# Attention 0: the order of values and scores in each unit of TensorE's program

## The chip, the cores and the metric

The kernel runs on one core of a Trainium2 chip. The metric is the device time of one execution in microseconds (us). The core has five engines that work side by side, each through its own list of instructions in order: TensorE (PE; its weight loads are shown apart as PEld), VectorE (DVE), ScalarE (ACT), GpSimd (POOL) and SyncE (SP), which only issues transfers. They wait for one another by semaphores.

## What is computed

Four layers act on `x` of 8 batches, 256 rows and 1024 columns: a cross attention with 32 heads and 8 key heads (attention 0), a linear layer with low-rank updates, a second cross attention and a linear layer in 8 bits. Only the first matters here. Its core, cut down:

```python
def _L0_xattn_ref(hidden_states, encoder_hidden_states, wq, wk, wv, wo, ln_w):
    x = _rmsnorm(hidden_states, ln_w)
    q = jnp.einsum('bqd,hd->bqh', x, wq).reshape(B, Qlen, N_HEADS, HEAD_DIM)
    k = jnp.einsum('bkd,hd->bkh', encoder_hidden_states, wk).reshape(B, Klen, N_KV_HEADS, HEAD_DIM)
    v = jnp.einsum('bkd,hd->bkh', encoder_hidden_states, wv).reshape(B, Klen, N_KV_HEADS, HEAD_DIM)
    ...
    scores = jnp.einsum('bhqd,bhkd->bhqk', q, k) / np.sqrt(HEAD_DIM).astype(np.float32)
    attn = jax.nn.softmax(scores.astype(jnp.float32), axis=-1).astype(q.dtype)
    out = jnp.einsum('bhqk,bhkd->bhqd', attn, v)
    ...
    return jnp.einsum('bqh,dh->bqd', out, wo)

x = x + jnp.tanh(g_xattn[0]) * _L0_xattn_ref(_layernorm(x, axis=-1), ctx_4096, ...)
```

## The kernel before

The program runs in stages, one behind the other: context (keys, values), attention 0 (`attn0_stage`), the output projection and first linear layer (`mid_stage`), attention 1, and the last linear layer. Attention 0 occupies about 181 to 688 us.

**Units.** Each batch has 16 units (`UNITS`): four heads (`t = n // 2`) times one half of the 256 rows (`qb = n % 2`). A unit goes through the engines in this way:

- scores (L956): TensorE multiplies queries with keys, 4 matmuls into the bank pair `n % 2` of `a_psS`;
- `maximum` (L1063): VectorE takes the negated row maximum of each head out of those banks;
- `exponentials` (L1148): ScalarE takes four exponentials, with their sums, into `a_prob`;
- `transposes` (L966): TensorE transposes the probabilities, 8 of 128x128, into `a_psT`; ScalarE (L1165) and in some units VectorE (L1108) copy them to `a_probT`;
- `values` (L979): TensorE multiplies them with the values into `a_psO`, 8 matmuls that the profile shows as 16 records. Each fills only 32 columns of the array. Behind the values of every odd unit come two more transposes (L985), which turn the reciprocals of the sums; GpSimd (L881) spreads these beforehand;
- `normalise_o` (L1076, L1078): VectorE multiplies the two and frees `a_psO` by `o_ready`, for which the values of the next even unit wait.

**The query step.** Each unit also carries a piece of the next batch's queries: in units 0 to 3 four transposes of x (L915), and from unit 4 on a half or a whole query tile of 12 or 24 matmuls (L931). All of them use the one bank `a_psQ`. VectorE empties it in a `split` of two instructions (L1056 and L1058: high and low part). Before it writes the bank again, TensorE waits for the second (`psQ_lo`). In the last batch no next one exists; the matmuls of the low-rank update stand there (L1006, from unit 4 on), with VectorE's `copy_update` (L1094) after each of four quarters.

**The order.** It is written out by hand, and each engine keeps it. TensorE in unit n of a batch, before:

```python
transposes(b, n)
if n + 2 < UNITS:
    scores(b, i, u, n + 2)
...
if n:
    values(b, u, n - 1)
if more:
    query_step(b + 1, 1 - u, n)
```

So scores run two units ahead and values one behind. VectorE's step n holds, in this order: the split (in step 0 the last of this batch; in steps 1 to 4, 5, 7, 8, 10, 11, 13 and 14 the next batch's), in odd steps from 5 the copy L1108, in odd steps the reciprocals L1113, `maximum(n + 2)`, in even steps `normalise_o(n // 2 - 1)`. While batches remain whose x is still to come (batches 0 to 5), step 6 adds the statistics of one tile (L590), step 9 the rest of them (L590, L607) and step 12 the normalisation (L644). In the last batch, each even step adds the low part of an output weight (L1068) instead, and steps 7, 10 and 13 a `copy_update` at their end. ScalarE's step n holds the copies of unit n and then the exponentials of unit n + 2.

Two batches stand in one round of a hardware loop of three rounds; the last two batches stand behind it.

Of the kernel before, what the change touches and what calls it, by code (L numbers as in the profile page):

```python
# [690 lines left out]
def attn0_stage(nc, sh, c, scratch, wq, rows, norm):  # L691
# [22 lines left out]
    with ExitStack() as es:  # L714
# [186 lines left out]
        def _(pe):  # L901
# [35 lines left out]
            def query_step(b, u, n):  # L937

                if n < XFILLS:
                    transposed_x(b, u, n)  # L940
                    return
                three, part = (n - XFILLS) // 3, (n - XFILLS) % 3
                if part == 0:
                    query(b, 2 * three, range(KT))
                else:
                    query(b, 2 * three + 1, range((part - 1) * KT // 2, part * KT // 2))

            def scores(b, i, u, n):

                t, qb = n // TT, n % TT  # L950
                if n % (UNITS // 2) == 0:
                    pe.wait_ge(q_stacked[t // QUAD], 16 * QUAD_DMAS * (b + 1) + 1)
                if n == 0:
                    pe.wait_ge(kv_loaded[u], 16 * 5 * (i + 1))
                for j in range(JH0):
                    last = nc.tensor.matmul(psS[:, 2 * (n % 2) + j // 2, (j % 2) * S:(j % 2 + 1) * S],  # L956
                                            q_stack[:, t, j, qb * P:(qb + 1) * P],
                                            k_stack[:, u, (t // REP0) * JH0 + j, :], start=True, stop=True)
                last.then_inc(scores_full, 1)

            def transposes(b, n):
                pe.wait_ge(exp_done, UNITS * b + n + 1)
                for kt in range(TT):
                    pe.wait_ge(psT_copied[kt], UNITS * b + n + 1)
                    for j in range(JH0):
                        last = nc.tensor.transpose(psT[:, kt, j * P:(j + 1) * P],  # L966
                                                   prob[:, n % 2, j, kt * P:(kt + 1) * P], ident[:, :])
                    last.then_inc(psT_full[kt], 1)

            def values(b, u, n):  # L970
                t, qb = n // TT, n % TT
                if qb == 0:
                    pe.wait_ge(o_ready, KT * b + t + 1)
                for kt in range(TT):
                    pe.wait_ge(psT_copied[kt], UNITS * b + n + 2)
                for kt in range(TT):
                    for j in range(JH0):
                        head = (t // REP0) * JH0 + j
                        nc.tensor.matmul(psO[j * HD0:(j + 1) * HD0, 0, qb * P:(qb + 1) * P],  # L979
                                         v0[:, u, kt, head * HD0:(head + 1) * HD0], probT[:, n % 2, kt, j, :],  # L980
                                         start=(kt == 0), stop=(kt == TT - 1))
                if qb == TT - 1:
                    pe.wait_ge(recip_ready, KT * b + t + 1)
                    for s in range(TT):
                        last = nc.tensor.transpose(psO[:, 1, s * P:(s + 1) * P],  # L985
                                                   recip[:, t % 2, s, :, :].rearrange("p j c -> p (j c)"), ident[:, :])
                    last.then_inc(psO_full, 1)
# [9 lines left out]
            def update_part(quarter, kt):  # L997

                if kt == 0:
                    if quarter == 0:  # L1000
                        pe.wait_ge(summed, 1)
                        pe.wait_ge(psQ_lo, Q_USES * B + 1)
                    else:
                        pe.wait_ge(update_copied, quarter)
                    pe.wait_ge(table_loaded[quarter % 2], 32 * (quarter // 2) + 32)
                last = nc.tensor.matmul(psQ[0:RR, 0:QUARTER], wsum[:, kt, :], table(quarter, kt // QUAD)[:, kt % QUAD, :],  # L1006
                                        start=(kt == 0), stop=(kt == KT - 1))
                if kt == KT - 1:
                    last.then_inc(update_full, 1)
# [5 lines left out]
            def body(i, final):  # L1015
                for u in range(2):
                    b = 2 * i + u
                    more = not (final and u == 1)
                    for n in range(UNITS):
                        transposes(b, n)  # L1020
                        if n + 2 < UNITS:
                            scores(b, i, u, n + 2)
                        elif more:
                            scores(b + 1, i + u, 1 - u, n + 2 - UNITS)
                        if n:
                            values(b, u, n - 1)
                        if more:
                            query_step(b + 1, 1 - u, n)
                        else:
                            for quarter, kt in update_steps.get(n, ()):  # L1030
                                update_part(quarter, kt)
                    values(b, u, UNITS - 1)

            with pe.Fori(0, PAIRS - 1) as i:
                body(i, False)
            body(PAIRS - 1, True)

        @block.vector
# [1437 lines left out]
```

## Time and profile before

| | us |
|---|---|
| median of 3 runs | 1495.08 |
| lowest and highest | 1495.05, 1495.64 |
| the profiled execution | 1496.8 |
| span of its instructions | 1495.1 |
| mean granted TensorE clock, share of full speed | 0.966 |

| engine | busy, us | share of the span |
|---|---|---|
| PE | 1377.2 | 92% |
| PEld | 1120.8 | 75% |
| DVE | 971.4 | 65% |
| ACT | 745.9 | 50% |
| POOL | 426.3 | 29% |

The views name an instruction by engine, line of the kernel and operation, then what it writes and what it reads (`a_psS<-a_k_stack,a_q_stack`), the shapes and the count. Matmuls are pipelined, and their ends in the trace are modelled: one that follows closely starts before the one ahead has ended, so on TensorE the distance from start to start is what counts. Busy time is a union over records and hides this. Where an engine was idle, the releaser is inferred from semaphore events.

### The profile page before, as it was taken

To read this page: it belongs to the slowest core of one execution; us is meant where nothing else is said; L and a number is where in the kernel's file an instruction comes from. 1 tells how busy PE (TensorE), PEld (TensorE's weight loads), DVE (VectorE), ACT (ScalarE), POOL (GpSimd) and SP (SyncE) were. 2 spreads that over 40 slices of the span, in tenths; PEclk is the share of its full clock that TensorE was granted. 3 is DMA by queue.
4 is the path that set the end of the run, shared out by engine and by line. 5 is a ranking of instruction groups with operands and counts; after the bars stand their busy time and mean duration, and the time that the engine had idled before them with its cause. 6 is when DMAs were issued, how large, how long until landed. Compare 5 with 4: busy or idle time off the path is not lost. (4 is left out here: it accounts for less than half of the span.)

```text
span 1495.1 us, 28528 instructions
## 1 busy us (share of the span) xinstructions
PE 1377.2 (92%) x10782; PEld 1120.8 (75%) x10782; DVE 971.4 (65%) x1564; ACT 745.9 (50%) x1881; POOL 426.3 (29%) x473
## 2 busy tenths in 40 slices
PE   6998789989989999987999999999779999999388
PEld 6998778979889898865888888888556666666144
DVE  4363277777767767565232256578567999998597
ACT  4231167766757767763111110113157777777396
POOL 0010001101010110010110232232358888887324
PEclk9999889999999999999999999999889999999789
DMA  6742454553544536464445452112332222221023
GB/s 224 244 155 85 90 126 117 139 146 77 145 110 120 147 96 167 125 197 150 166 167 197 157 210 99 56 36 84 113 81 65 62 64 64 63 64 43 1 85 141
DMA packets 127910, 174.93 MB, mean 117 GB/s; under 512 B 27799, under 2 KB 96919, under 8 KB 127792
## 3 DMA queue, kind: packets, MB, share of 16 engines
q1 hardware_dynamic: 127792, 173.26, 39.9%
q8 instruction: 86, 1.41, 0.4%
q14 instruction: 32, 0.26, 0.1%
HBM read 86.94 MB, written 35.29 MB: 82 GB/s over the span
## 5 line engine op out<-in xcount | busy, mean ns | idle before, releaser
L1148 ACT ACTIVATE a_prob<-a_psS,a_negmax 128x256 f32<-128x256 f32 x512 | 236.7, 483 | 158.6 <-DVE a_negmax L1063 158.4
L1063 DVE TENSOR_REDUCE a_negmax<-a_psS 128x4 f32<-128x1024 f32 x128 | 154.1, 1204 | 68.1 <-PE a_psS L956 66.5
L881 POOL COPY a_recip<-a_recip_head 128x256 f32<-128x256 f32 x64 | 25.6, 400 | 526.5 <-DVE a_recip_head L1113 526.5
L931 PE MATMUL a_psQ<-a_xT_hi,wide 128*128 128x256 f32 x912 | 170.9, 288 | 0.4
L1375 PE MATMUL m_psY<-wide,m_a_hi 128*128 128x512 f32 x512 | 159.3, 393 | 6.8 <-DVE m_a_lo L1423 6.8
L1375 PE MATMUL m_psY<-w_ffn,m_a_hi 128*128 128x512 f32 x512 | 158.3, 390 | 0.0
L966 PE MATMUL a_psT<-ident,a_prob 128*128 128x128 f32 x1024 | 138.0, 279 | 14.1 <-issue 6.1
L931 PEld LDWEIGHTS a_psQ<-a_xT_hi,wide 128*128 128x128 f32 x912 | 138.7, 189 | 9.1 <-issue 5.9
L1165 ACT COPY a_probT<-a_psT 128x512 f32<-128x512 f32 x208 | 115.8, 609 | 36.7 <-PE a_psT L966 35.6
L966 PEld LDWEIGHTS a_psT<-ident,a_prob 128*128 128x128 f32 x1024 | 116.7, 143 | 23.0 <-issue 12.7
L931 PE MATMUL a_psQ<-a_xT_lo,wide 128*128 128x256 f32 x456 | 127.5, 280 | 0.0
L1375 PEld LDWEIGHTS m_psY<-wide,m_a_hi 128*128 128x128 f32 x512 | 96.8, 189 | 27.5 <-DVE m_a_lo L1423 7.0
L1375 PEld LDWEIGHTS m_psY<-w_ffn,m_a_hi 128*128 128x128 f32 x512 | 95.6, 188 | 19.5
L1148 ACT ACTIVATION_READ_ACCUMULATOR a_prob<-a_psS,a_negmax 128x1 f32 x512 | 109.4, 214 | 0.0
L2115 ACT ACTIVATE b_prob<-b_prob 128x1024 f32<-128x1024 f32 x64 | 67.9, 1061 | 79.1 <-DVE b_prob L1989 79.1
L1375 PE MATMUL m_psY<-wide,m_a_lo 128*128 128x512 f32 x256 | 100.2, 392 | 0.0
L1375 PE MATMUL m_psY<-w_ffn,m_a_lo 128*128 128x512 f32 x256 | 99.7, 389 | 0.0
L956 PE MATMUL a_psS<-a_k_stack,a_q_stack 128*128 128x256 f32 x512 | 94.1, 307 | 2.9 <-issue 2.9
L1983 DVE TENSOR_REDUCE b_maxes<-b_psS 128x16 f32<-128x1024 f32 x64 | 77.9, 1217 | 27.1 <-PE b_psS L1891 26.0
L1901 PEld LDWEIGHTS b_psT<-ident,b_prob 128*128 128x128 f32 x512 | 60.2, 142 | 35.2 <-issue 32.9
L931 PEld LDWEIGHTS a_psQ<-a_xT_lo,wide 128*128 128x128 f32 x456 | 85.7, 188 | 0.0
L1820 POOL TENSOR_TENSOR b_halves<-b_prob 128x512 f32<-128x512 f32 x64 | 82.5, 1290 | 6.6 <-ACT b_prob L2115 6.0
(233 smaller groups left out, 3013.9 us busy)
## 6 DMA issues: line engine op xcount, KB each, us to landing
a_q_stack<-a_q_hi SPq DMA_DIRECT2D x128, 128.0 KB, 2.6
a_q_stack<-a_q_lo SPq DMA_DIRECT2D x128, 128.0 KB, 2.6
c_raw<-lay_ctxT SPq DMA_DIRECT2D x16, 512.0 KB, 4.8
rows<-in_x SPq DMA_DIRECT2D x8, 1024.0 KB, 6.4
scratch_o<-a_oT SPq DMA_DIRECT2D x16, 512.0 KB, 3.0
m_x<-in_x SPq DMA_DIRECT2D x8, 1024.0 KB, 5.9
scratch_x<-m_x SPq DMA_DIRECT2D x8, 1024.0 KB, 5.1
b_q_stack<-b_q_hi SPq DMA_DIRECT2D x64, 128.0 KB, 2.3
```

The source lines that it names most:

```text
L881: nc.gpsimd.tensor_copy(recip[:, t % 2], recip_head[:, t % 2].unsqueeze(3).broadcast_to([P, TT, JH0, HD0])).then_inc(recip_ready, 1)
L931: last = nc.tensor.matmul(bank[:, 0:S], w[:, kt, t * P:(t + 1) * P], a[:, kt, :], start=(kt == 0 and w is wq.hi and a is xT_hi), stop=(kt ...
L956: last = nc.tensor.matmul(psS[:, 2 * (n % 2) + j // 2, (j % 2) * S:(j % 2 + 1) * S], q_stack[:, t, j, qb * P:(qb + 1) * P], k_stack[:, u, ...
L966: last = nc.tensor.transpose(psT[:, kt, j * P:(j + 1) * P], prob[:, n % 2, j, kt * P:(kt + 1) * P], ident[:, :])
L1063: nc.vector.tensor_reduce(negmax[:, n % 2, :], psS[:, bank:bank + 2, :].rearrange("p a (j k) -> p (a j) k", k=S), AX_X, ALU.max, negate=Tr ...
L1148: last = nc.scalar.activation(prob[:, n % 2, j, :], psS[:, 2 * (n % 2) + j // 2, (j % 2) * S:(j % 2 + 1) * S], ACT.Exp, bias=negmax[:, n % ...
L1165: nc.scalar.copy(probT[:, n % 2, kt, :, :], psT[:, kt, :].rearrange("p (j q) -> p j q", j=JH0)).then_inc(psT_copied[kt], 1)
L1375: last = nc.tensor.matmul(psY[:, 2 * t + h, :], a[:, u, kt, rows_t], m[:, kt, cols], start=(kt == 0 and a is a_hi and m is w.hi), stop=(kt ...
L1820: nc.gpsimd.tensor_tensor(halves[:, n % 2], unit[:, :, 0:NK1 // 2], unit[:, :, NK1 // 2:NK1], ALU.add).then_inc(halves_ready, 1)
L1901: last = nc.tensor.transpose(psT[:, t, j * P:(j + 1) * P], prob[:, n % 2, (4 * t + j) * P:(4 * t + j + 1) * P], ident[:, :])
L1983: nc.vector.tensor_reduce(maxes[:, n % 2, :], psS[:, n % 2, :].rearrange("p (h k) -> p h k", h=NH1), AX_X, ALU.max).then_inc(max_ready, 1)
L2115: nc.scalar.activation(prob[:, n % 2, :], prob[:, n % 2, :], ACT.Exp).then_inc(exp_done, 1)
```

## The change

In every unit except the first of each batch (which has no values) TensorE now runs the values of the unit one back ahead of the scores of the unit two on. Nothing else is touched; all semaphore counts stay.

```diff
                     for n in range(UNITS):
                         transposes(b, n)
+                        if n:
+                            values(b, u, n - 1)
                         if n + 2 < UNITS:
                             scores(b, i, u, n + 2)
                         elif more:
                             scores(b + 1, i + u, 1 - u, n + 2 - UNITS)
-                        if n:
-                            values(b, u, n - 1)
                         if more:
                             query_step(b + 1, 1 - u, n)
                         else:
```

TensorE's list in unit 6 of a batch in the loop, an even unit, where the two transposes of reciprocals go along with the values. The rows named ISA and REGISTER_ALU are waits and their counting.

```order
 L962 REGISTER_ALU
 L966 MATMUL a_psT<-ident,a_prob 128x128 x8
+L979 MATMUL a_psO<-a_probT,a_v 32x128 x8
+L985 MATMUL a_psO<-ident,a_recip 128x128 x2
 L952 ISA
 L956 MATMUL a_psS<-a_k_stack,a_q_stack 128x256 x4
-L979 MATMUL a_psO<-a_probT,a_v 32x128 x8
-L985 MATMUL a_psO<-ident,a_recip 128x128 x2
 L931 MATMUL a_psQ<-a_xT_hi,wide 128x256 x2
 L931 MATMUL a_psQ<-a_xT_lo,wide 128x256
```

The scores, with the wait for the stacked queries in front of them, now stand behind the values and the reciprocals, and directly ahead of the query step.

TensorE's list in unit 7, an odd unit, which starts a new query tile:

```order
 L962 REGISTER_ALU
 L966 MATMUL a_psT<-ident,a_prob 128x128 x8
-L956 MATMUL a_psS<-a_k_stack,a_q_stack 128x256 x4
 L973 REGISTER_ALU
 L979 MATMUL a_psO<-a_probT,a_v 32x128 x8
+L956 MATMUL a_psS<-a_k_stack,a_q_stack 128x256 x4
 L925 REGISTER_ALU
 L931 MATMUL a_psQ<-a_xT_hi,wide 128x256 x2
```

The scores have moved behind the values and behind the wait for `o_ready` (L973) in front of those. The lists of the other engines are the same as before.

## Rows read from the trace of the kernel before

**Rows 1.** Busy time by engine, batch 5 from unit 1 on; clock, DMA at the end.
```profile
505.98:564.74 58.76, 58.14 (x658) 52.18 (x657) 42.75 (x74) 42.51 (x151) 5.62 (x15) 1.00 0.51 130
```

**Rows 2.** Waits of TensorE's loads, 195 to 690 us: total, times, longest.
```profile
PEld a_psQ L1006 <- DVE a_update L1094: 6.1, 3, 2.9
...
PEld a_psQ L931 <- DVE a_q_lo L1058: 3.2, 12, 0.3
```

**Rows 3.** Timeline of TensorE, batch 5, unit 6: start us, duration us, instruction.
```profile
523.04 0.39 PE L931 MATMUL a_psQ<-a_xT_hi,wide 128*128 128x256 f32 x2
...
524.18 0.71 PE L956 MATMUL a_psS<-a_k_stack,a_q_stack 128*128 128x256 f32 x4
524.82 0.64 PE L979 MATMUL a_psO<-a_probT,a_v 128*32 128x128 f32 x16
525.40 0.44 PE L985 MATMUL a_psO<-ident,a_recip 128*128 128x128 f32 x2
525.59 0.50 PE L931 MATMUL a_psQ<-a_xT_hi,wide 128*128 128x256 f32 x2
```

**Rows 4.** Timeline of TensorE, other joints: batch 5, unit 6; batch 7; batch 2, unit 0.
```profile
523.82 0.60 PE L966 MATMUL a_psT<-ident,a_prob 128*128 128x128 f32 x4
...
680.14 0.60 PE L966 MATMUL a_psT<-ident,a_prob 128*128 128x128 f32 x4
680.67 0.64 PE L979 MATMUL a_psO<-a_probT,a_v 128*32 128x128 f32 x16
...
316.78 0.72 PE L956 MATMUL a_psS<-a_k_stack,a_q_stack 128*128 128x256 f32 x4
317.34 0.27 PE L915 MATMUL a_psQ<-ident,rows 128*128 128x128 f32 x1
```

**Rows 5.** Timeline of TensorE, batch 5, unit 7: values and start of the query.
```profile
528.52 0.65 PE L979 MATMUL a_psO<-a_probT,a_v 128*32 128x128 f32 x16
529.09 0.39 PE L931 MATMUL a_psQ<-a_xT_hi,wide 128*128 128x256 f32 x1
```

**Rows 6.** Timeline of VectorE, batch 5, steps 6 and 7; idle time in brackets.
```profile
524.93 1.23 DVE L1063 TENSOR_REDUCE a_negmax<-a_psS 128x4 f32<-128x1024 f32 x1 [2.07 <-PE a_psS L956]
...
526.52 0.42 DVE L1078 TENSOR_TENSOR a_oT<-a_psO,a_recipT 128x256 f32<-128x256 f32 x1
...
528.50 0.42 DVE L1058 TENSOR_TENSOR a_q_lo<-a_psQ,a_q_hi 128x256 fp32r<-128x256 f32 x1
```

**Rows 7.** Timelines of VectorE and TensorE, batch 5, units 12 and 13.
```profile
549.35 1.22 DVE L1063 TENSOR_REDUCE a_negmax<-a_psS 128x4 f32<-128x1024 f32 x1 [2.18 <-PE a_psS L956]
...
553.17 0.42 DVE L1058 TENSOR_TENSOR a_q_lo<-a_psQ,a_q_hi 128x256 fp32r<-128x256 f32 x1
...
553.65 0.50 PE L931 MATMUL a_psQ<-a_xT_hi,wide 128*128 128x256 f32 x2
```

**Rows 8.** Timelines of VectorE and TensorE, batch 5, units 2 and 3.
```profile
510.72 1.22 DVE L1063 TENSOR_REDUCE a_negmax<-a_psS 128x4 f32<-128x1024 f32 x1 [0.32 <-PE a_psS L956]
...
513.37 0.69 DVE L1058 TENSOR_TENSOR a_xT_lo<-a_psQ,a_xT_hi 128x512 fp32r<-128x512 f32 x1
...
514.11 0.66 PE L915 MATMUL a_psQ<-ident,rows 128*128 128x128 f32 x4
```

**Rows 9.** Timelines of VectorE and TensorE, batch 5, unit 10.
```profile
540.38 0.42 DVE L1058 TENSOR_TENSOR a_q_lo<-a_psQ,a_q_hi 128x256 fp32r<-128x256 f32 x1
...
541.38 0.48 PE L931 MATMUL a_psQ<-a_xT_hi,wide 128*128 128x256 f32 x2
```

**Rows 10.** The exponentials, from the page's costliest groups: busy us, mean ns, idle.
```profile
L1148 ACT ACTIVATE a_prob<-a_psS,a_negmax 128x256 f32<-128x256 f32 x512 | 236.7, 483 | 158.6 <-DVE a_negmax L1063 158.4
```

**Rows 11.** Timeline of VectorE, batch 7, steps 6 and 7.
```profile
646.08 1.23 DVE L1063 TENSOR_REDUCE a_negmax<-a_psS 128x4 f32<-128x1024 f32 x1 [2.27 <-PE a_psS L956]
...
650.94 0.40 DVE L1094 TENSOR_SCALAR a_update<-a_psQ 40x256 f32<-40x256 f32 x1
```

**Rows 12.** Busy time around the start of batch 4; the granted clock is third last.
```profile
441.00:444.30 3.30, 2.88 (x14) 2.91 (x15) 0.05 (x1) 1.17 (x2) 0.00 (x0) 0.50 0.86 243
445.00:505.00 60.00, 59.18 (x667) 53.03 (x664) 43.84 (x77) 43.60 (x154) 5.62 (x15) 1.00 0.44 110
```

## The prediction

> **What bounds the kernel now.** I read three views of the stretch from 181 to 688 us, in which attention 0 runs its 128 units. First the busy table of one batch, 505.98 to 564.74 us [rows 1]. TensorE's matmuls fill 58.14 of 58.76 us. VectorE has 42.75 and ScalarE 42.51, so each is idle for some 16 us. TensorE is the bound, and nothing else is. Work that is only moved on TensorE costs nothing there; what can cost is a new idle stretch on it. Second the list of waits of TensorE's loads [rows 2]: it waits for VectorE in a few short places, among them for `a_q_lo` (12 times, 3.2 us) and, in the last batch, for `a_update` (3 times, 6.1 us). So VectorE has little time in hand somewhere. Third the timeline around those places, where the reader should look at the gap between the end of the releasing VectorE instruction and the start of the waiting matmul.
>
> Names: T(n), S(n+2), V(n-1), R and Q(n) are the transposes of the probabilities, the scores, the values, the two transposes of reciprocals behind every second V, and the query step. Unit n of a batch ran T, S, V, (R), Q and will run T, V, (R), S, Q. R stands where n is even. Batches are 0 to 7; the rows below are of batch 5 unless another is named.
>
> **The cost on TensorE itself.** The parts are the same; the joints between them change. T into S: S starts at 524.18 [rows 3] and the last four transposes at 523.82 [rows 4], 0.36 us ahead. T into V: the same four start 0.53 us ahead of V (680.14 to 680.67, in a unit without scores) [rows 4]. So T into V costs 0.17 more. S into V is 0.64 from start to start, V into R 0.58, R into Q 0.19 [rows 3], V into Q 0.57 (528.52 to 529.09) [rows 5]. S into a query step, which no unit of the steady state had, is seen once a batch in unit 0, where nothing stands between: 316.78 to 317.34, 0.56 [rows 4]. An even unit from S's old place to Q's start: before 0.64 + 0.58 + 0.19 = 1.41; after 0.17 + 0.58 + 0.19 + 0.56 = 1.50. That is 0.09 more, but the first pair of query matmuls takes 0.50 us behind V or R and 0.39 behind matmuls of its own kind [rows 3], and S is of that kind: 0.11 back. Sum: nothing, with bounds of 0.1 us on either side for each of 111 units, or 11 us. I take zero, since the same two joints (out of a transpose, out of V) remain in number and only their neighbours change.
>
> The Trainium skill ("TensorE: Matmul & The Clock Gate", Part 3, The mechanism) says that a weight load overlaps matmuls in flight only where it goes to another row group. V's loads fill 32 columns over all rows, and the joint of 0.17 us is what that rule would give; by it the gap is moved and not removed, as in my sum.
>
> **What moves: the scores.** S starts later by what is now ahead of it. Even units: 0.17 + 0.58 + 0.19 = 0.94 us. Odd units: 0.17 + 0.57 = 0.74, and 0.02 for its own slower first matmul out of V, 0.76. V comes 0.64 - 0.17 = 0.47 earlier. No semaphore wait is added for V: T(n) waits for the same copies of the unit before. Behind S stands VectorE's row maximum (L1063), and VectorE works through its list in order: behind maximum(n+2) are queued, in even steps, `normalise_o`, statistics (step 6) or the normalisation (step 12), and then the split of the next step, for which the next Q waits. So a later maximum can stop TensorE one unit later. Unit by unit:
>
> Unit 6 into 7. The maximum of step 6 starts at 524.93, straight behind S, after 2.07 us of idle time; from there L1076, L1078, L590, L1056 and L1058 run without a gap until 528.50 + 0.42 = 528.92 [rows 6]. Q(7) starts at 529.09 [rows 5]: 0.17 in hand, of which a handoff needs 0.06 (next paragraph). The whole chain moves by 0.94. Cost 0.94 - 0.11 = **0.83 us**.
>
> Unit 12 into 13. Maximum at 549.35 behind S (2.18 idle), then the normalisation, and the split ends at 553.17 + 0.42; Q(13) starts at 553.65, at once [rows 7]. This is already a wait, so nothing is in hand: **0.94 us**.
>
> Unit 2 into 3. Maximum at 510.72 behind S (0.32 idle), the split ends at 513.37 + 0.69 = 514.06, Q(3) starts at 514.11 [rows 8]: **0.94 us**. Here V(2) also waits for `normalise_o` of that delayed step, with S(5) behind it. From there V and S take 0.06 + 0.57 + 0.56 = 1.19 us to Q(3), while VectorE's split takes two instructions of some 0.69, 1.4 us; so the split ends last and V's wait costs nothing more.
>
> Unit 9 into 10. The maximum of step 9 comes behind an odd unit's S, 0.76 later; the split ends at 540.38 + 0.42 = 540.80 and Q(10) starts at 541.38 [rows 9]: 0.58 - 0.06 = 0.52 in hand, cost **0.24 us**.
>
> All other units keep a margin. T's own wait for the exponentials is loose in the long units: maximum(8) ended at 526.16 [rows 6], four activations of 0.48 [rows 10] end by 528.1, and T(8) stands behind Q(7), which only starts at 529.09 and runs for some 2.8 us; 0.94 fits. In the short units 2 to 4 the exponentials are closer to their T, but the 0.94 us stall of unit 3 gives ScalarE the time back. The wait for `o_ready` ahead of V in odd units is the narrowest: `normalise_o` of step 6 ended at 526.52 + 0.42 = 526.94 [rows 6] and V began at 528.52 [rows 5], 1.58 apart; it shrinks by 0.94 + 0.47 = 1.41 to 0.17, and 0.06 is needed. It just holds.
>
> A stall of TensorE isn't made up, as TensorE is full. Per batch 0.83 + 0.94 + 0.94 + 0.24 = 2.95 us. Batches 0 to 5 have all four: 17.7. In batch 6 no x is left to normalise, so only the stall of unit 3 remains: 0.9.
>
> **Batch 7** has no query steps; the update's matmuls stand there, and each new quarter waits for VectorE's copy of the last. The maximum of step 6 waited 2.27 us for S and started at 646.08; behind it a queue without a wait ends with the copy at 650.94 + 0.40, where the quarter's matmuls, the next on TensorE, wait for it [rows 11]. The chain moves by 0.94; the same in units 10 and 13 (three waits of 6.1 us in all [rows 2]): 2.8 us. In its units 2 to 4, which have no query step to cover anything, I let a later S(4) delay T(4) through the exponentials by its whole 0.94; that is an estimate by the same figure, between nothing and 2 us. Together 3.8.
>
> Sum: 17.7 + 0.9 + 3.8 = 22.4 us in the stage, and the stages behind it start at its end. The profiled execution had 1496.8 us for a span of 1495.1; the median of the three runs, 1495.08, is 1.7 below its time. The added stalls don't depend on that offset, so 1495.1 + 22.4 = **1517.5 us**.
>
> **The clock.** From 441.0 to 444.3 us the granted clock was 0.50, the lower level of 1.2 GHz, at the start of the loop's third round; from 445 on it is 1.00 [rows 12]. 3.3 us at half speed can cost 1.65 at most. TensorE had stood idle just before, at the loop's turn. With the stage's idle stretches moved and lengthened, one or two such spells more or fewer are possible: 3 us on either side. The skill's page on the clock gate ("Why this matters for your kernels") warns of idle gaps of this length; by it the new stalls of under 1 us each leave the clock alone.
>
> **Rivals.**
> 1. *The joints on TensorE cost more than thought.* If S behind V and Q behind S cost 0.1 us a unit, the upper bound above, 111 units add 11 us: 1529. For it: no row shows V straight into S. Against: V into Q, V into R and S into a query step are all seen. Chance 0.10.
> 2. *VectorE catches up part of the delay.* If the maximum doesn't move by the full 0.94 or some queued work slips ahead of S, half the stalls remain: 1506. Against: every one of the four chains starts with VectorE idle and waiting for S, and its order is fixed. Chance 0.10. That nothing is seen at all would need margins near 0.9 us where [rows 5 to 8] show 0.17 us in hand and none: 1495, chance 0.03.
> 3. *Faster.* V behind T shares its joint, and S flows into Q without one. If T into V cost no more than T into S (0.17 saved) and S into Q saved another 0.12 through its warm pipeline, each of 111 units would gain 0.29 us, 32 in all, and with the 22.4 of stalls the result is 10 us faster, 1485. It decides from 0.2 us a unit. Against: the 0.53 us of [rows 4]. Chance 0.04.
>
> **How the numbers follow.** The forecast (1510 to 1526) has 0.73. Together with a part of rivals 1 and 2 the range that holds the time 8 times in 10 is 1508 to 1528: below are half of rival 2, no change and faster, above is half of rival 1. Measurements of this kernel can tell about 0.2%, 3 us, from no change. Slower by more: 0.73 + 0.10 + 0.10 = 0.93; same 0.03; faster 0.04.
>
> **What the changed profile would show.** S starts 0.94 (even) or 0.76 (odd) later behind T, V 0.47 earlier. TensorE's waits for `a_q_lo` and `a_xT_lo` grow by 0.8 to 0.9 us each in units 3, 7 and 13 of batches 0 to 5, and none appear in units 7 and 13 of batch 6. The period of units 8, 9, 11, 12, 14 is as before (within 0.1). The wait for `a_update` grows by 2.8. Matmul time of TensorE is unchanged. I am wrong if the waits stay and the units themselves lengthen (rival 1), if V of units 7, 9, 13 and 15 waits for `a_oT` by more than 0.1 us, or if the time comes from a later stage.

## The result and the profile after

The changed kernel takes 1519.92 us in the median (1518.44 to 1521.48), the one before 1495.07 (1494.56 to 1495.64). The ratio is 1.0166, with a 95% interval of 1.0149 to 1.0184: 24.9 us slower, where 22.4 were forecast. The profiled execution of the changed kernel had 1518.44 us and a span of 1516.7, which is 21.6 more than the span before. The three other executions of the changed kernel took 1.0 to 3.0 us longer, at a mean granted clock of 0.965 against 0.970 in the profiled one; what the traces below add up to belongs to the 21.6 and not to the 24.9. The matmuls of the stage behind attention 0 begin at 715.4 us in place of 693.4, 22.0 later, and at the end the spans differ by 21.6, so the whole loss lies in attention 0 and 0.4 us come back behind it.

TensorE's order in unit 6 and at the start of unit 7 of batch 5, from the timeline of the changed kernel (start, duration, instruction). It answers to [rows 3, 5]. In all views `...` stands for lines left out.

```profile
535.39 1.04 PE L966 MATMUL a_psT<-ident,a_prob 128*128 128x128 f32 x8
536.35 0.65 PE L979 MATMUL a_psO<-a_probT,a_v 128*32 128x128 f32 x16
536.93 0.44 PE L985 MATMUL a_psO<-ident,a_recip 128*128 128x128 f32 x2
537.12 0.72 PE L956 MATMUL a_psS<-a_k_stack,a_q_stack 128*128 128x256 f32 x4
537.68 0.40 PE L931 MATMUL a_psQ<-a_xT_hi,wide 128*128 128x256 f32 x2
...
539.10 1.03 PE L966 MATMUL a_psT<-ident,a_prob 128*128 128x128 f32 x8
540.06 0.65 PE L979 MATMUL a_psO<-a_probT,a_v 128*32 128x128 f32 x16
540.63 0.74 PE L956 MATMUL a_psS<-a_k_stack,a_q_stack 128*128 128x256 f32 x4
541.92 0.38 PE L931 MATMUL a_psQ<-a_xT_hi,wide 128*128 128x256 f32 x1 [0.55 <-DVE a_q_lo L1058]
```

Every joint (the time from the start of one kind of matmul to the start of the next) is as summed: transposes to values 0.96, values to reciprocals 0.58, reciprocals to scores 0.19, scores to query 0.56. The scores start 1.73 us behind the transposes of their unit; before it was 0.79. The first pair of query matmuls behind scores takes 0.40 us and not 0.50. Unit 6 as a whole lasts 3.71 us (535.39 to 539.10), and before 3.69. In unit 7 the bracket is the new thing: matmuls idle for 0.55 us until VectorE's `a_q_lo`, where [rows 5] had no bracket.

VectorE behind the later scores, in steps 6 and 7 of the same batch (compare [rows 6]):

```profile
537.88 1.23 DVE L1063 TENSOR_REDUCE a_negmax<-a_psS 128x4 f32<-128x1024 f32 x1 [2.45 <-PE a_psS L956]
...
539.47 0.42 DVE L1078 TENSOR_TENSOR a_oT<-a_psO,a_recipT 128x256 f32<-128x256 f32 x1
539.81 1.27 DVE L590 BATCH_NORM_STATS2 norm_stats<-rows 128x6 f32<-128x512 f32 x2
...
541.44 0.42 DVE L1058 TENSOR_TENSOR a_q_lo<-a_psQ,a_q_hi 128x256 fp32r<-128x256 f32 x1
```

The maximum starts 537.88 - 535.39 = 2.49 us behind the start of unit 6's transposes. Before, those began at 523.39 and the maximum at 524.93, 1.54 behind, which is 0.95 less than now. The split ends at 541.86 and TensorE goes on at 541.92. Step 12 and unit 13 show the same chain with the longer normalisation:

```profile
563.39 1.23 DVE L1063 TENSOR_REDUCE a_negmax<-a_psS 128x4 f32<-128x1024 f32 x1 [2.48 <-PE a_psS L956]
...
567.21 0.42 DVE L1058 TENSOR_TENSOR a_q_lo<-a_psQ,a_q_hi 128x256 fp32r<-128x256 f32 x1
...
567.69 0.51 PE L931 MATMUL a_psQ<-a_xT_hi,wide 128*128 128x256 f32 x2 [0.81 <-DVE a_q_lo L1058]
```

The list of waits of TensorE's loads over the stage (total, times, longest), answering to [rows 2]:

```profile
PEld a_psS L956 <- issue: 12.3, 62, 0.2
PEld a_psQ L931 <- DVE a_q_lo L1058: 11.9, 18, 1.0
PEld a_psO L979 <- DVE a_oT L1078: 11.4, 38, 1.0
PEld a_psQ L1006 <- DVE a_update L1094: 8.1, 3, 3.8
```

`a_q_lo` went from 3.2 us to 11.9: 18 waits are those of units 7, 10 and 13 of six batches. `a_update` went from 6.1 to 8.1, 2.0 us more and not the 2.8 of the forecast. The other two lines have to be read with care. The 62 waits of 0.2 us ahead of the scores are the joint behind the values, which stood ahead of the query before. Nearly all of the 38 on `a_oT` are the joint between transposes and values, laid to the semaphore that happened to be asked for there; TensorE's matmuls themselves wait for it 7 times, in unit 3 of batches 1 to 7 (below).

Start to start of transposes, changed kernel less the one before, in us, by unit of three batches without a disturbance of the clock at their start:

| unit | 2 | 3 | 4 | 7 | 8 | 10 | 13 | 14 | others | whole batch |
|---|---|---|---|---|---|---|---|---|---|---|
| batch 1 | 0.16 | 0.65 | -0.12 | 0.80 | -0.06 | 0.18 | 0.94 | -0.06 | 0.26 | 2.75 |
| batch 5 | 0.17 | 0.64 | -0.14 | 0.89 | -0.01 | 0.14 | 0.85 | -0.01 | 0.03 | 2.56 |
| batch 6 | 0.24 | 0.58 | -0.05 | 0.08 | -0.01 | 0.00 | 0.08 | 0.00 | 0.05 | 0.97 |

Units 3, 7, 10 and 13 carry the loss; what unit 2 adds, unit 4 mostly gives back. Over batches 0 to 6 it is 16.3 us in this trace, in batch 7 it is 7.1. The first unit had begun 1.5 us earlier than in the profile before, which leaves the 22.0 above. At the loop's turns the clock moved time about: unit 0 was 1.57 us longer in batch 2 and 1.38 shorter in batch 4.

### The profile page after: what moved, and what is told of

The parts are those of the page before. It is cut to its first block and busy times, and to the rows that moved or that the text cites. A ratio compares the mean times of both kernels' runs of the same rounds, so it can differ in the third digit from the quotient of the medians.

```text
span 1516.7 us, 28520 instructions
## 1 busy us (share of the span) xinstructions
PE 1379.9 (91%) x10774; PEld 1115.4 (74%) x10782; DVE 975.3 (64%) x1564; ACT 744.9 (49%) x1881; POOL 426.2 (28%) x473
## 5 line engine op out<-in xcount | busy, mean ns | idle before, releaser
L931 PE MATMUL a_psQ<-a_xT_hi,wide 128*128 128x256 f32 x912 | 163.6, 280 | 8.2 <-DVE a_q_lo L1058 8.1
L931 PEld LDWEIGHTS a_psQ<-a_xT_hi,wide 128*128 128x128 f32 x912 | 138.5, 188 | 11.9 <-DVE a_q_lo L1058 11.9
L966 PEld LDWEIGHTS a_psT<-ident,a_prob 128*128 128x128 f32 x1024 | 117.0, 144 | 24.9 <-issue 14.4
L931 PE MATMUL a_psQ<-a_xT_lo,wide 128*128 128x256 f32 x456 | 127.1, 279 | 0.0
L1148 ACT ACTIVATION_READ_ACCUMULATOR a_prob<-a_psS,a_negmax 128x1 f32 x512 | 104.6, 204 | 0.0
L979 PE MATMUL a_psO<-a_probT,a_v 128*32 128x128 f32 x2048 | 82.8, 280 | 4.4 <-DVE a_oT L1078 4.3
L931 PEld LDWEIGHTS a_psQ<-a_xT_lo,wide 128*128 128x128 f32 x456 | 85.6, 188 | 0.0
```

The source lines that it names most:

```text
L931: last = nc.tensor.matmul(bank[:, 0:S], w[:, kt, t * P:(t + 1) * P], a[:, kt, :], start=(kt == 0 and w is wq.hi and a is xT_hi), stop=(kt ...
L966: last = nc.tensor.transpose(psT[:, kt, j * P:(j + 1) * P], prob[:, n % 2, j, kt * P:(kt + 1) * P], ident[:, :])
L1148: last = nc.scalar.activation(prob[:, n % 2, j, :], psS[:, 2 * (n % 2) + j // 2, (j % 2) * S:(j % 2 + 1) * S], ACT.Exp, bias=negmax[:, n % ...
```

## The experiments

Each was timed beside the kernel before, on the same chip within a group. The ratios are to that kernel's runs. Medians of the kernel before were 1494.38 in the first group (experiments 1 to 4), 1494.04 in the second (5, 6, 7 and 9) and 1494.05 in the third (8 and 10). Of each kernel one execution has a trace.

**1. Values first everywhere but in four units.**

```diff
+values_first = n not in ((2, 6, 9, 12) if more else (2, 6, 10, 12))
+if n and values_first:
+    values(b, u, n - 1)
 if n + 2 < UNITS:
     scores(b, i, u, n + 2)
...
-if n:
+if n and not values_first:
     values(b, u, n - 1)
```

> The kernel before with the values put first in every unit except those whose scores start one of the four chains that ended in a stall: units 2, 6, 9 and 12 (2, 6, 10 and 12 in the last batch). 83 of 111 units with both parts are swapped. If the cost is VectorE's delayed queue, nearly all of the 24.9 us goes: 1496 to 1499 us, and TensorE's waits for a_q_lo are back near 3.2 us. If the joints between kinds of matmuls on TensorE cost it, three quarters stay: about 1513. If it is the values' own earlier place (their wait for a_oT), it stays too.

Measured: 1497.35 us, ratio 1.0013 (0.9998 to 1.0027). Nearly all of the loss is gone, though three quarters of the swaps are in. (Units with both parts are 118 and not 111 as forecast and expectation have it: 15 in each of seven batches and 13 in the last; 86 are swapped here.) In the trace 1.9 us are left. Most of it stands in unit 2 (0.16 us in batches 1, 3 and 5, 0.73 to 0.78 in 0, 2 and 4), where the transposes of unit 3 wait for ScalarE behind the later scores of unit 1, as in batch 2:

```profile
325.54 0.63 PE L966 MATMUL a_psT<-ident,a_prob 128*128 128x128 f32 x4 [0.56 <-ACT a_probT L1168]
```

In the changed kernel the same delay and that of unit 3 don't add: where one is whole, the other is small (0.73 and 0.01 in batch 0, 0.16 and 0.65 in batch 1). In batch 7 the swaps cost some 2.1 us, and some 2.0 came back, since the two spells of the lower clock in that batch before (from 632.1 and from 666.2) are missing.

**2. Values first in those four units only.** The same edit with `n in` for `n not in`.

> The kernel before with the values put first only in units 2, 6, 9 and 12 (2, 6, 10 and 12 in the last batch), 32 units of 127. VectorE's delayed queue: nearly all of the cost is there, 1515 to 1520 us, with stalls of about 0.7, 0.8, 0.2 and 0.9 us in units 3, 7, 10 and 13 of batches 0 to 5. Joints on TensorE: a quarter of it, about 1501.

Measured: 1521.86 us, ratio 1.0171 (1.0152 to 1.0190). All of the loss is there, with a quarter of the swaps. Waits of TensorE's loads in the first kernel, then in the second:

```profile
PEld a_psS L956 <- issue: 10.9, 55, 0.2
...
PEld a_psQ L1006 <- DVE a_update L1097: 6.5, 3, 2.9
...
```

```profile
PEld a_psQ L931 <- DVE a_q_lo L1061: 15.8, 18, 1.3
...
PEld a_psQ L1006 <- DVE a_update L1097: 8.9, 3, 3.8
...
PEld a_psQ L915 <- DVE a_xT_lo L1061: 8.0, 12, 0.9
...
PEld a_psS L956 <- issue: 1.4, 7, 0.2
```

In the first kernel TensorE's loads no longer wait for `a_q_lo` ahead of a query tile (L931) at all, while the joint behind the values stands 55 times ahead of the scores at no cost. In the second the joint is there 7 times and the waits are at their largest. So moving the joints is free here, and what costs is the delay of the scores at the head of VectorE's four chains.

**3. Reciprocals behind the scores,** on the changed kernel:

```diff
 if n:
     values(b, u, n - 1)
 if n + 2 < UNITS:
     scores(b, i, u, n + 2)
...
+if n:
+    reciprocals(b, n - 1)
```

where `reciprocals` holds the wait and the two transposes of L985, taken out of `values`.

> The changed kernel with the two transposes of reciprocals put behind the scores: transposes, values, scores, reciprocals, query. The scores of an even unit are then late by the values alone, 0.75 us in place of 0.94. VectorE's delayed queue: the stalls of units 3, 7 and 13 shrink by 0.18 us each, 3 to 4 us in all, so about 1516. If only the order of values and scores matters and not the length of what is ahead, no change against the changed kernel, 1520. One joint more on TensorE (scores into transposes) could cost up to 0.1 us in 64 units, 6 us.

Measured: 1518.48 us, ratio 1.0136 (1.0105 to 1.0168), 1.4 us under the changed kernel. The times alone don't tell 1516 from 1520. The trace does: TensorE's two stalls of batch 5 are here

```profile
544.97 0.51 PE L931 MATMUL a_psQ<-a_xT_hi,wide 128*128 128x256 f32 x2 [0.33 <-DVE a_q_lo L1064]
...
570.56 0.50 PE L931 MATMUL a_psQ<-a_xT_hi,wide 128*128 128x256 f32 x2 [0.59 <-DVE a_q_lo L1064]
```

0.33 and 0.59 us, against 0.55 and 0.81: 0.22 less each, for scores that come 0.19 us earlier. What that gave back, the additional joint took: most even units are 0.04 us longer, and 0.1 where the second tile of a pair starts (units 8 and 14). Over all units the two traces differ by 0.1 us, so the time shows nothing of the 3 to 4 us expected; the shorter stalls do.

**4. The other direction: scores ahead of the transposes.**

```diff
-transposes(b, n)
+pe.wait_ge(exp_done, UNITS * b + n + 1)
 if n + 2 < UNITS:
     scores(b, i, u, n + 2)
...
+transposes(b, n)
 if n:
     values(b, u, n - 1)
```

The wait is the one that `transposes` began with; it also guards the banks that the scores write.

> The other direction: scores, transposes, values, query. The scores' maximum starts some 0.8 us earlier than in the kernel before, in every unit. VectorE's delayed queue: the small waits of the kernel before shrink (units 13, 7 and the update's three waits), 1490 to 1494 us. If the joints decide, the order has as many of them as the one before: 1495. If the transposes' later place hurts instead (ScalarE's copies come 0.6 us later, and in units 2 to 4 ScalarE is the bound), slower by some us: 1498 to 1502.

Measured: 1491.2 us, ratio 0.9971 (0.9955 to 0.9987). TensorE's loads wait 1.2 us for `a_q_lo` (6 times) and 5.9 for `a_update`:

```profile
PEld a_psQ L1005 <- DVE a_update L1094: 5.9, 3, 2.7
...
PEld a_psQ L931 <- DVE a_q_lo L1058: 1.2, 6, 0.2
```

Earlier scores give time, which fits, but not in the way that I had expected. Units 7 and 13 of batches 0 to 6 changed by 0.15 us at most, so next to nothing came from VectorE's splits. The largest single piece was in unit 1, 0.47 us in most batches, which I had not named: in the kernel before TensorE waits for ScalarE's copies ahead of the transposes of unit 2 (0.50 us at 509.15 in batch 5), and here it doesn't. Another 2.1 us of the 6.6 that the trace gained are in batch 7, where two spells of the lower clock are missing, though the waits for `a_update` are nearly as before.

**5. Values first in the last batch only.** The edit of the first experiment with `values_first = not more`.

> The kernel before with the values put first in the last batch alone, where the update's matmuls stand in place of the query step. The term of the prediction: four delays of 0.94 us, 3.8 us, 1499. By the profile of the changed kernel (7.1 us in this batch, with one more spell of the lower clock) it is 6 to 8 us: 1501 to 1502. Anything near 1495 would put that batch's cost on what came before it.

Measured: 1503.91 us, ratio 1.0051 (1.0032 to 1.0070), 9.9 us slower, more than either figure; in the trace that batch is 9.5 us longer. Of TensorE's clock in this kernel, by stretches (span, then busy time and count by engine, then the granted clock, DMA share and GB/s):

```profile
655.00:658.20 3.20, 3.20 (x26) 2.35 (x26) 0.00 (x0) 1.36 (x4) 0.00 (x0) 0.50 0.04 15
668.60:675.30 6.70, 5.58 (x30) 3.13 (x30) 1.86 (x4) 1.37 (x5) 0.75 (x2) 0.50 0.42 143
685.70:688.90 3.20, 3.20 (x12) 1.71 (x10) 0.00 (x0) 1.20 (x6) 0.00 (x0) 0.50 0.70 241
699.30:706.00 6.70, 3.89 (x9) 3.12 (x10) 2.50 (x4) 3.25 (x6) 0.10 (x1) 0.50 0.55 151
```

The first three, 13.1 us, lie at or just behind the waits of units 7, 10 and 13 and ran at the lower of the two levels. The fourth lies behind the batch; such a stretch stands there in the kernel before (from 690.1) and the changed one (from 712.2) too, some 7 us behind the start of the last transposes. In the changed kernel the spell of unit 10 lasted 3.4 us and not 6.8, and there was none in unit 2, where this kernel and the one before have one.

**6. Changed kernel, the normalisation's pieces ahead of the maximum.**

```diff
+if n == 6 and not final:
+    dve.wait_ge(x_loaded[u], 16 * i + 16)
+    norm.stats_of(x[:, u], 0)
+if n == 9 and not final:
+    norm.moments_of(dve, b + 2, x[:, u], last_tile_only=True)
+if n == 12 and not final:
+    norm.normalise(dve, b + 2, x[:, u], x[:, u], norm.STEPS_RMS)
 if n + 2 < UNITS:
     maximum(b, n + 2)
...
-if n == 6 and not final:
...
```

> The changed kernel, with VectorE's extra pieces (statistics in step 6, the rest of them in step 9, the normalisation in step 12) put ahead of the maximum in their steps instead of behind it. They then fill the time in which VectorE waits for the later scores. Late queue behind the maximum as cause of the stalls: those of units 7, 10 and 13 vanish in batches 0 to 5, 6 x (0.80 + 0.19 + 0.94) = 11.6 us, about 1508; unit 3's stall and the last batch's stay. If the stalls came from the scores being late for anything else, the time stays at 1520.

Measured: 1514.81 us, ratio 1.0130 (1.0109 to 1.0150): 5 us regained and not 12. By units, the stalls of 7 and 10 vanished but for 0.08 us (0.72 and 0.18 to 0.21 us less in each of the batches 0 to 4, 0.81 and 0.15 in batch 5), but of unit 13's only 0.04 to 0.38 went. VectorE in step 12, and TensorE in unit 13:

```profile
557.22 1.54 DVE L644 TENSOR_SCALAR rows<-rows,norm_moments,norm_rstd 128x1024 f32<-128x1024 f32 x2 [1.87 <-POOL norm_rstd L638]
558.67 1.22 DVE L1063 TENSOR_REDUCE a_negmax<-a_psS 128x4 f32<-128x1024 f32 x1
...
560.25 0.42 DVE L1078 TENSOR_TENSOR a_oT<-a_psO,a_recipT 128x256 f32<-128x256 f32 x1
```

```profile
560.73 0.64 PE L979 MATMUL a_psO<-a_probT,a_v 128*32 128x128 f32 x16 [0.65 <-DVE a_oT L1078]
```

The normalisation waited for GpSimd's result until 557.22, ended at 558.76 and so pushed the maximum itself and `normalise_o` back; now the values of unit 13 wait for `o_ready`, 0.65 us. The stall had changed its place, from the split to `normalise_o`. The queue as cause of the stalls of 7 and 10 is shown. My expectation failed in step 12, since it took the piece to fill idle time without asking when its input is there.

**7. Kernel before, copy of the update ahead of the maximum.**

```diff
+if n > UPDATE_STEP and (n - UPDATE_STEP) % 3 == 0 and not more:
+    copy_update((n - UPDATE_STEP) // 3 - 1)
 if n + 2 < UNITS:
     maximum(b, n + 2)
...
-if n > UPDATE_STEP and (n - UPDATE_STEP) % 3 == 0 and not more:
-    copy_update((n - UPDATE_STEP) // 3 - 1)
```

> The kernel before with the last batch's copy of the update put ahead of the maximum in steps 7, 10 and 13. If TensorE's 6.1 us of waits for a_update come from that copy's place in VectorE's queue, they shrink by 1.1 us in units 7 and 13 and by up to 2.9 in unit 10, about 5 us in all: 1490. If the spell of the lower clock at 666 us hangs on the long wait of unit 10, it goes too, and with it 1 to 1.5 us more. If the tables' transfers set these waits, no change.

Measured: 1489.87 us, ratio 0.9966 (0.9951 to 0.9981). The wait and the clock of the middle of batch 7:

```profile
PEld a_psQ L1006 <- DVE a_update L1094: 1.0, 2, 0.5
```

```profile
636.00:680.00 44.00, 43.51 (x442) 28.73 (x440) 30.84 (x47) 31.36 (x110) 9.71 (x14) 1.00 0.64 189
```

The kernel before had a clock of 0.96 over the same stretch and 0.50 from 666.3 to 669.5. Units 7, 10, 11 and 13 are shorter by 1.13, 2.70, 1.51 and 1.13 us. Unit 11 has no wait for `a_update`; its 1.51 us are the spell that no longer comes. The spell of unit 2 (from 632.1 before) came here too, from 631.9.

**8. Changed kernel, the same copy ahead.**

> The changed kernel with the last batch's copy of the update ahead of the maximum in steps 7, 10 and 13. The changed kernel lost 7.1 us in that batch, the last-batch-only kernel 9.5, where four delays of 0.94 were 3.8; in both traces three spells of the lower clock lie on the three long waits for a_update. If those waits bring the spells about, this kernel loses both: the waits (8.1 us in all) shrink to under 3, the spells in units 7, 10 and 13 are gone, and the last batch is shorter by 8 to 12 us than in the changed kernel: 1508 to 1512. If the spells come regardless of the waits, 5 us: 1515.

Measured: 1507.83 us, ratio 1.0086 (1.0064 to 1.0107), 12 us better than the changed kernel. The last batch is 3.6 us shorter than before and 10.7 shorter than in the changed kernel, with no spell in it:

```profile
638.00:698.00 60.00, 54.95 (x561) 37.48 (x554) 38.06 (x58) 42.42 (x150) 11.50 (x17) 1.00 0.63 176
```

The waits for `a_update` shrank by 8.1 - 2.0 = 6.1 us; the other 4.6 us go with the three spells (3.4 us each at half speed, 1.7 at most if TensorE is busy throughout). It stays 13.8 us above the kernel before, which is the stalls of batches 0 to 6 less the gain in the last.

**9. Scores first and everything early,** the edits of 4, 6 and 7 together on the kernel before.

> Scores ahead of the transposes, and on VectorE both the normalisation's pieces and the copy of the update ahead of the maximum. The gains should add: 3 us of the scores' place and 5 of the copy, less what the pieces ahead of the maximum delay it, since with earlier scores VectorE has no long idle time there: 1486 to 1490.

Measured: 1488.52 us, ratio 0.9952 (0.9935 to 0.9968). The gains nearly add, but unit 13 of batches 0 to 5 is 0.45 to 0.77 us longer, for the reason found in 6.

**10. Scores first, only the copy early,** the edits of 4 and 7.

> Scores ahead of the transposes and the copy of the update ahead of the maximum, the normalisation's pieces left where they were. In the kernel with everything early unit 13 of each batch lost 0.45 to 0.77 us to the values' wait for a_oT behind the 1.5 us normalisation; here that is gone, 3 us less than its 1488.5: 1485 to 1487. If the pieces' place didn't matter: 1488 to 1489.

Measured: 1486.35 us, ratio 0.9933 (0.9919 to 0.9948), 7.7 us faster than the kernel before and 33.6 faster than the changed one. Unit 13's loss is gone. The difference to 9 (2.2 us) lies near the spread of the runs; the unit times of the two traces, not the medians, are what shows it.

## Why the prediction was right, and where not

**TensorE's own parts: nothing.** Held. The joints measured 0.96, 0.58, 0.19 and 0.56 us; experiment 1 has them in 86 units with the time unchanged within 0.3%. The bound of 11 us was not needed, and rival 1 is out. The rule on weight loads that the prediction quoted from the Trainium skill ("TensorE: Matmul & The Clock Gate", Part 3, The mechanism) was not put to a test: no run changed the rows that a load fills. By itself it doesn't single out the joint into the values either, since the transposes' loads fill all 128 rows too (128*128 against 128*32 in the views).

**The four chains.** Held in mechanism, in place and mostly in size. The sum had per batch:

| stall | forecast | batch 1 | batch 5 |
|---|---|---|---|
| unit 7 | 0.83 | 0.80 | 0.89 |
| unit 13 | 0.94 | 0.94 | 0.85 |
| unit 10 | 0.24 | 0.18 | 0.14 |
| units 2 to 4 | 0.94 | 0.69 | 0.67 |

The term of unit 3 was too large by a quarter of a us. The query step of unit 3 did start late by the whole amount, as these rows of the changed kernel show (batch 5):

```profile
522.99 1.22 DVE L1063 TENSOR_REDUCE a_negmax<-a_psS 128x4 f32<-128x1024 f32 x1 [0.82 <-PE a_psS L956]
...
525.06 0.65 PE L979 MATMUL a_psO<-a_probT,a_v 128*32 128x128 f32 x16 [0.56 <-DVE a_oT L1078]
...
526.38 0.66 PE L915 MATMUL a_psQ<-ident,rows 128*128 128x128 f32 x4
526.87 0.38 PE L966 MATMUL a_psT<-ident,a_prob 128*128 128x128 f32 x2
```

But the next transposes follow 0.49 us behind that query step, and before it was 0.63 ([rows 8], with these transposes at 514.74). There they had come 0.15 us behind the end of ScalarE's copy (514.59), as at 509.15 where a wait is shown (copy until 509.00), and not behind the query step; the stall gave ScalarE the time. Another 0.12 came back in unit 4. I had said that ScalarE catches up inside the added time, and had not taken that off the sum. The values' wait for `o_ready` in unit 3 was 0.56 us and cost nothing more, as said.

**Other units keep a margin.** Held in batches 0 to 6: units 8, 9, 11, 12, 14 and 15 changed by 0.1 us at most (batch 1's unit 15, at the loop's turn, by 0.2). The narrow margin of the values in unit 7, 0.17 us, was 0.17: `normalise_o` ended at 539.89 and they began at 540.06. In units 7 and 13 of batch 7 it was not enough: there the values start 1.19 and 1.18 us behind the transposes, against 1.02 in the units beside them.

**Batch 6: only unit 3.** Held (0.97 us against 0.9).

**Batch 7: 3.8 us.** Wrong in size: 7.1 in the profile, 9.9 alone (experiment 5). The step that failed is the one that put the clock at nothing in the sum, as a matter apart with 3 us on either side. The chain moved by 0.95 us as forecast: from the start of unit 6's transposes (659.97; before 644.48) to the update's first matmul it was 7.87 us (667.84), and before 6.92 (651.40). Then the matmuls themselves ran slower. Before, and after:

```profile
651.40 1.49 PE L1006 MATMUL a_psQ<-a_q_hi,a_wsum 128*40 128x256 f32 x6 [1.35 <-DVE a_update L1094]
```

```profile
667.84 2.78 PE L1006 MATMUL a_psQ<-a_q_hi,a_wsum 128*40 128x256 f32 x6 [1.95 <-DVE a_update L1094]
```

```profile
667.90:671.10 3.20, 3.20 (x9) 1.45 (x10) 0.00 (x0) 1.53 (x8) 0.03 (x1) 0.50 1.09 402
685.00:688.20 3.20, 3.20 (x19) 2.06 (x21) 0.80 (x2) 0.23 (x1) 0.11 (x1) 0.50 0.22 72
698.60:701.90 3.30, 3.30 (x9) 1.55 (x10) 0.00 (x0) 1.58 (x8) 0.08 (x1) 0.50 0.79 276
```

Six matmuls took 2.78 us in place of 1.49, since the granted clock had fallen to 0.50, the 1.2 GHz level, just when TensorE came out of its longer wait. A spell came at all three waits, in units 7, 10 and 13, where the kernel before had one such spell (behind the wait of unit 10) and one in unit 2. The 7.1 us are then the three chains with 2.8, units 2 to 4 with 0.4 (in the kernel before the spell is among them), units 5 and 9 with 0.2 each, and 3.4 in units 7, 8, 10, 11, 13 and 14 beyond the chains: three spells in place of one.

That the waits bring the spells about is shown for the changed kernel: all three are in its trace and in experiment 6's, where the last batch is the same, and none in experiment 8, where the waits are cut. For the kernel before it is not shown. Its spell behind unit 10 is gone in experiment 7, but it is gone as well in experiment 1, behind a wait as long as before (the kernel before, then experiment 1):

```profile
664.87 1.49 PE L1006 MATMUL a_psQ<-a_q_hi,a_wsum 128*40 128x256 f32 x6 [2.62 <-DVE a_update L1094]
```

```profile
666.75 1.06 PE L1006 MATMUL a_psQ<-a_q_hi,a_wsum 128*40 128x256 f32 x4 [2.62 <-DVE a_update L1097]
...
636.00:690.00 54.00, 45.11 (x443) 29.14 (x442) 33.28 (x50) 32.37 (x114) 9.72 (x14) 1.00 0.56 162
```

In experiment 3 waits of the same length in units 7 and 13 differ, the first without a spell and the second with one:

```profile
670.68 1.49 PE L1009 MATMUL a_psQ<-a_q_hi,a_wsum 128*40 128x256 f32 x6 [1.89 <-DVE a_update L1100]
700.61 1.88 PE L1009 MATMUL a_psQ<-a_q_hi,a_wsum 128*40 128x256 f32 x5 [1.89 <-DVE a_update L1100]
...
666.50:683.00 16.50, 13.42 (x133) 9.02 (x132) 10.50 (x17) 10.81 (x39) 2.77 (x4) 1.00 0.65 227
701.20:704.50 3.30, 3.30 (x13) 1.95 (x10) 0.00 (x0) 1.49 (x6) 0.00 (x0) 0.50 0.63 217
```

Over all traces, none of the six waits of 1.3 to 1.6 us in units 7 and 13 had a spell with it (kernel before, experiments 1 and 4), and nine of the ten of 1.9 to 2.3 us had one (changed kernel, experiments 2, 3, 5 and 6). So a longer wait makes a spell likelier, but its length alone doesn't decide. What else does stays open.

**The sum.** 16.3 + 7.1 = 23.4 us in the trace, against 18.6 + 3.8 = 22.4: the chains of batches 0 to 6 a little smaller, the last batch nearly twice as large. The two errors, 2.3 us too much and 3.3 too little, have opposite signs, and that the total is nearer than its parts is luck.

**The rivals.** That VectorE catches up half is out by the stalls' sizes, 0.79 to 0.97 us in units 7 and 13 of batches 0 to 5, and experiment 2 has the whole loss from the four heads of the chains. Faster through cheaper joints is out by the joints' measured lengths.

**Of the clock,** I had written that by the Trainium skill ("TensorE: Matmul & The Clock Gate", "Why this matters for your kernels") stalls of under 1 us leave it alone. In batches 0 to 6 the trace agrees: the stalls of 0.5 to 0.8 us in units 3, 7 and 13 left the clock at 1.00 (batch 5 below), and the one spell between 194 and 667 us, from 319.7, is at the loop's turn. In batch 7 the measurement goes beyond it: spells came at waits of 1.95, 3.56 and 1.94 us, the first and last of them shorter than the idle gaps that the section warns of.

```profile
517.30:578.63 61.33, 58.91 (x658) 51.80 (x657) 43.26 (x74) 41.64 (x148) 5.64 (x15) 1.00 0.49 124
```

## What to carry to other kernels

On the engine that was full here, moving work cost nothing; the price is read on the engine that the moved result feeds. Find where that engine sits idle until exactly this result, follow its list from there without a gap, and see who waits at the end: the delay less the slack at that end is the loss (0.79 to 0.97 us in units 7 and 13, where the sum had 0.83 and 0.94). Where the end keeps a margin, as in units 8, 9, 11, 12 and 14 of batches 0 to 6, it is 0.1 us at most. To shorten such a chain, move the feeding work earlier or lift what is urgent ahead of the wait, but ask of each lifted piece when its own input is there. And where the engine is only partly busy, as in the last batch, leave room in the forecast for the clock.

## What the runs showed of the hardware

- A wait of TensorE can cost more than its length, when the clock falls with it. In unit 7 of the last batch 0.95 us of delay came with 1.3 us of slower matmuls (2.78 against 1.49 us for the same six), and taking the waits away gave 6.1 us of waiting and 4.6 more. But waits of one length were followed by the lower level in one place and not in another (2.62 us in the kernel before and in experiment 1, 1.89 us twice in experiment 3). At the loop's turns it was the same: the kernel before lost the clock at the start of batch 4 and not of batch 2, the changed one the other way round (319.7 to 323.1 us at 0.5), and unit 0 was 1.38 us shorter in batch 4 and 1.57 longer in batch 2.
- At the full clock TensorE's matmuls start 0.17 us later behind transposes when they are of the kind that fills 32 columns (0.53 against 0.36 us behind the same four transposes). Behind such matmuls its loads stand idle for 0.2 us, ahead of the reciprocals' transposes (64 times), scores (62 times in the changed kernel) and query matmuls (30 times in experiment 5).
